# Shared expert's first half: down products of rounded halves, chunk by chunk into four banks, and the first row transposes in the up products' bank

## What is computed

```python
def _L0_ffn_ref(x, Wg, W1, b1, W11, b11, W2, b2, Ws1, bs1, Ws11, bs11, Ws2, bs2):
    ...
    logits = xf @ Wg
    _, topi = jax.lax.top_k(logits, K)
    ...
    z = jax.nn.silu(xf @ Ws1 + bs1) * (xf @ Ws11 + bs11) @ Ws2 + bs2
    return (y + z).reshape(b, t, d)
x = x + jnp.tanh(g_xattn[0]) * _L0_xattn_ref(_layernorm(x, axis=-1), ctx_1024, ctx_1024, ...)
x = x + jnp.tanh(g_ffn[0]) * _L0_ffn_ref(_layernorm(x, axis=-1), L0_ffn_Wg, ...)
```

## Time and profile before

| What | Value |
|---|---|
| Median of three runs | 577.51 us (574.35, 577.51, 577.92) |
| The profiled execution, its time | 574.41 us |
| Its span in the profile | 572.2 us |
| TensorE busy in it | 546.9 us (96%) |
| VectorE, ScalarE, POOL busy | 352.1, 238.2, 335.4 us |
| Mean granted TensorE clock | 0.997 of full speed |

### The profile page before, as it was taken

How to read it: one execution, slowest core, us unless ns; L and a number is a source line. 1 busy time by engine, 2 the same in 40 slices (tenths; PEclk the granted TensorE clock), 3 DMA queues, 4 the chain that set the end, 5 groups by cost and what they waited for, 6 DMA issues and landing times.

```text
span 572.2 us, 12049 instructions
## 1 busy us (share of the span) xinstructions
PE 546.9 (96%) x3290; PEld 442.1 (77%) x3291; DVE 352.1 (62%) x861; ACT 238.2 (42%) x787; POOL 335.4 (59%) x273
## 2 busy tenths in 40 slices
PE   8879999999988999988999999999999999999997
PEld 7546766767757878767888888888888888888886
DVE  6648788778668842145566555665556655535687
ACT  0799899999995211012222212222122221233232
POOL 4588899999864386640374675364454560226660
PEclk9899999999999999999999999999999999999999
DMA  8572001001023044244257868558556210012442
GB/s 282 236 295 80 21 21 37 21 18 37 12 82 111 30 165 175 92 129 175 69 190 262 302 240 302 177 179 289 201 173 258 82 46 29 28 56 84 121 121 89
DMA packets 32898, 76.08 MB, mean 133 GB/s; under 512 B 4960, under 2 KB 21856, under 8 KB 29920
## 3 DMA queue, kind: packets, MB, share of 16 engines
q1 hardware_dynamic: 14960, 52.44, 25.7%
q10 hardware_dynamic: 14832, 14.82, 8.2%
q0 software_dynamic: 3072, 8.39, 4.7%
HBM read 54.93 MB, written 18.61 MB: 129 GB/s over the span
## 4 chain that ended last, share of the span: by engine, by line
PE 85%; ACT 6%; DVE 5%; issue 3%; POOL 0%; ACTq 0%; DVEq 0%; POOLq 0%
PE mid L748 14%; PE big L729 8%; PE big L731 8%; PE big L730 7%; PE big L652 5%; PE big L650 5%; PE big L651 5%; PE big L516 5%; PE mid L739 4%; ACT arena L836 3%; PE mid L529 3%; PE work L548 3%; PE last L541 2%; PE last L669 2%; PE work L669 2%
## 5 line engine op out<-in xcount | busy, mean ns | idle before, releaser
L936 ACT ACTIVATE last<-arena 128x512 f32<-128x512 f32 x47 | 28.3, 602 | 183.4 <-DVE arena L1405 183.4
L836 ACT ACTIVATE arena<-big,nmax 128x128 f32<-128x128 f32 x256 | 90.0, 388 | 1.7 <-DVE nmax L1058 1.5
L748 PE MATMUL mid<-dring,arena 128*128 x376 | 89.0, 379 | 0.0
L1405 DVE TENSOR_TENSOR arena<-big,bring 128x512 f32<-128x512 f32 x47 | 32.5, 692 | 87.3 <-PE big L731 87.3
L729 PE MATMUL big<-u_hi,xsT_hi 128*128 x188 | 81.8, 435 | 1.8 <-issue 1.8
L1568 POOL TENSOR_TENSOR u_lo<-arena,u_hi 128x2048 fp32r<-128x2048 f32 x16 | 74.3, 4645 | 1.3
L748 PEld LDWEIGHTS mid<-dring,arena 128*128 128x128 f32 x376 | 67.8, 190 | 7.3
L731 PE MATMUL big<-u_hi,xsT_lo 128*128 x188 | 73.5, 391 | 0.0
L730 PE MATMUL big<-u_lo,xsT_hi 128*128 x188 | 73.4, 390 | 0.0
L1544 POOL TENSOR_TENSOR arena<-arena,rinv 128x1024 f32<-128x1024 f32 (+1 forms) x32 | 59.4, 1855 | 13.5 <-DVE rinv L1066 13.5
L1668 POOL TENSOR_TENSOR pool_mark<-mhalf 128x1 f32<-128x1 f32 x15 | 2.9, 193 | 104.9 <-PE big L731 88.3
(11 more groups left out here) (197 smaller groups left out, 1203.8 us busy)
## 6 DMA issues: line engine op xcount, KB each, us to landing
arena<-up_w_dram SPq DMA_DIRECT2D x16, 1024.0 KB, 7.6
bring<-expert_bias_dram SPq DMA_DIRECT2D x16, 640.0 KB
dring<-down_w_dram SPq DMA_DIRECT2D x18, 512.0 KB
sorted_y<-arena ACTq DMA_DIRECT2D x47, 128.0 KB, 1.7
arena<-sorted_x ACTq DMA_DIRECT2D x43, 128.0 KB, 2.1
sorted_x<-dring SPq DMA_DIRECT2D x3, 1536.0 KB, 8.5
arena<-ctx_t_dram ACTq DMA_DIRECT2D x8, 256.0 KB, 2.7
dring<-up_w_dram SPq DMA_DIRECT2D x2, 1024.0 KB, 4.9
```

The costliest lines, as they stand in the source:

```text
L748: i = mm(mid[:, 1, 0:D], gT[:, p, c, :], dring[:, slot, c * D:(c + 1) * D], start=(c == 0), stop=(c == HC - 1))
L836: i = nc.scalar.activation(probs[:, u % 2, h, :], big[:, u % 2, h // 4, (h % 4) * CTX:(h % 4 + 1) * CTX], ACT.Exp, bias=nmax[:, u % 2, h:h ...
L1405: v.tensor_tensor(hb1[:, p, :], big[:, p, 0, :], bring[:, slot, 0:HID], ALU.add).then_inc(h1_ready, 1)
```

## The change

In the first half the down products are made as in the second: ScalarE rounds each hidden chunk, VectorE makes the remainder, and TensorE adds 12 products of 256 columns per chunk into four banks (`first_bank`). POOL makes the halves of the first half's down weights ahead of the scatter. The hidden chunks of the first half now go through `gg` (two buffers) in place of `gshT`; the new tiles `first_d` and `first_gs` lie in the region of `arena`. The totals and ranks go to free columns of `mid`, whose banks now hold down sums. TensorE's order becomes up n, down n - 1 (later n - 2). The transposes of the first two blocks of rows go into `big`, the up products' bank, ahead of down chunks 13 to 15, and these come ahead of the first block's up product. Functions common to both halves replace `last_down`; the order of the second half is as it was.

```diff
+        first_d = sb("first_d", [P, 2, DCOLS], F32R)
+        first_gs = sb("first_gs", [P, 2, 2, 512], F32R)
...
+        first_bank = (work, last, mid[:, 0, :], mid[:, 1, :])
+        def hidden_chunk(n):
+            return gg[:, n % 2, :] if n < HC * TILES // GROUP else gshT[:, n // HC % 2, n % HC, :]
+        def rounded_chunk(n):
+            if n < HC * TILES // GROUP:
+                return first_gs[:, 0, n % 2, :], first_gs[:, 1, n % 2, :]
+            return gs_hi[:, n % 2, :], gs_lo[:, n % 2, :]
...
-            def shared_down(s, tiles=range(GROUP)):
...
-                        i = mm(zbank[t % 2][:, 0:D], gshT[:, s % 2, c, t * P:(t + 1) * P], dring[:, slot, c * D:(c + 1) * D],
-                               start=(c == 0), stop=(c == HC - 1))
-                    i.then_inc(z_ps, 1)
+            def shared_down(n):
+                h, c = divmod(n, HC)
...
+                pe.wait_ge(gs_lo_ready, n + 1)
+                if n == 0:
+                    pe.wait_ge(d_split, 1)
+                    pe.wait_ge(lg_taken, PAIRS)
+                    pe.wait_ge(rank_taken, 1)
...
+                for t in range(GROUP):
+                    if c == 0 and h > 0:
+                        pe.wait_ge(z_taken, GROUP * (h - 1) + t + 1)
...
+                    mm(banks[t][:, 0:D], g_hi, w_hi, start=(c == 0), stop=False)
+                    mm(banks[t][:, 0:D], g_hi, w_lo, start=False, stop=False)
+                    i = mm(banks[t][:, 0:D], g_lo, w_hi, start=False, stop=(c == HC - 1))
+                    if c == HC - 1:
+                        i.then_inc(z_ps, 1)
+                    elif t == GROUP - 1:
+                        i.then_inc(gs_used, 1)
...
             shared_up(0, 3)
+            shared_down(0)
             pe.wait_ge(xfT_kept, 4)
...
+            for n in range(4, 8):
+                shared_up(1, n - 4)
+                shared_down(n - 3)
+            shared_down(5)
             pe.wait_ge(xfT_kept, PAIRS)
...
+            for n in range(8, 15):
+                shared_up(n // HC, n % HC)
+                shared_down(n - 2)
...
-            transpose_rows(0, 0)
-            shared_down(3, range(1))
-            transpose_rows(1, 1)
+            shared_up(3, 3)
+            pe.wait_ge(gsh_ready, HC * TILES // GROUP - 1)
+            transpose_rows(0, 0, big[:, 0, 0, :])
+            transpose_rows(1, 1, big[:, 0, 1, :])
+            for n in range(13, 16):
+                shared_down(n)
+            pe.wait_ge(xsT_ready, 2)
+            pe.wait_ge(gsh_ready, HC * TILES // GROUP)
             up(0, 0)
-            pe.wait_ge(xsT_ready, 2)
-            shared_down(3, range(1, GROUP))
-            pe.wait_ge(z_taken, 4 * GROUP)
+            pe.wait_ge(z_taken, TILES)
             transpose_rows(2, 2)
...
+            shared_silu(0, 0)
+            round_hidden(0)
+            shared_silu(0, 1)
+            round_hidden(1)
+            shared_silu(0, 2)
+            for n in range(3, 8):
+                shared_silu(n // HC, n % HC)
+                round_hidden(n - 1)
+            round_hidden(7)
+            for n in range(8, 16):
+                shared_silu(n // HC, n % HC)
+                round_hidden(n)
...
             v.tensor_tensor(gtmp[:, 0, :], top2[:, 1, :], top2[:, 0, :], ALU.subtract).then_inc(gate_exp_in, 1)
+            keep_rest(0)
             shared_hidden(0, [2])
...
             v.tensor_copy(pos[:, :, :], pos_f[:, :, :]).then_inc(pos_ready, 1)
+            keep_rest(1)
             shared_hidden(0, [3])
+            keep_rest(2)
             shared_hidden(1, [0])
+            keep_rest(3)
...
+            for n in range(8, 15):
+                shared_hidden(n // HC, [n % HC])
+                if n % HC == 1:
+                    add_shared(n // HC - 1)
+                keep_rest(n)
+            shared_hidden(3, [3])
+            copy_rows(0, 0, big[:, 0, 0, :])
+            keep_rest(15)
+            copy_rows(1, 1, big[:, 0, 1, :])
+            add_shared(3)
...
+            def split_down(n, source, hi, lo):
+                g.tensor_copy(hi, source).then_inc(d_hi_done, 1)
+                pool.wait_ge(d_hi_done, n)
+                g.tensor_tensor(lo, source, hi, ALU.subtract).then_inc(d_split, 1)
+
+            pool.wait_ge(w_even, 32)
+            pool.wait_ge(pt_ready, 2 * UNITS * PAIRS)
+            split_down(1, dring[:, 0, :], first_d[:, 0, :], first_d[:, 1, :])
             pool.wait_ge(pos_ready, 1)
```

More of the change, by code:

```diff
@@ L148, in flamingo_layer @@
         ARENA = 16128
-        arena = sb("arena", [P, ARENA])
+        with nc.sbuf_tensor("arena", [P, ARENA], F32) as whole:
+            arena = whole
+        first_d = sb("first_d", [P, 2, DCOLS], F32R)
+        first_gs = sb("first_gs", [P, 2, 2, 512], F32R)
+        sb("arena_rest", [P, ARENA - 2 * DCOLS - 4 * 512])
         taken = [0]
@@ L654, in shared_up @@
                     i.then_inc(sh_ps, 1)
[L656 to L671 removed]
+            def shared_down(n):
+                h, c = divmod(n, HC)
+                second = h >= TILES // GROUP
+                banks = last_bank if second else first_bank
+                hi, lo = rounded_chunk(n)
+                d = (d_hi, d_lo) if second else (first_d[:, 0, :], first_d[:, 1, :])
+                pe.wait_ge(gs_lo_ready, n + 1)
[3 more added lines that the diff above has]
+                    pe.wait_ge(rank_taken, 1)
+                if n == HC * TILES // GROUP:
+                    pe.wait_ge(d_split, 2)
+                    pe.wait_ge(g_ready, BLOCKS)
+                    pe.wait_ge(xsT_ready, BLOCKS)
+                    pe.wait_ge(gT_ready, BLOCKS)
+                    pe.wait_ge(y_ready, BLOCKS)
+                for t in range(GROUP):
+                    if c == 0 and h > 0:
+                        pe.wait_ge(z_taken, GROUP * (h - 1) + t + 1)
+                    g_hi, g_lo = hi[:, t * P:(t + 1) * P], lo[:, t * P:(t + 1) * P]
+                    w_hi, w_lo = d[0][:, c * D:(c + 1) * D], d[1][:, c * D:(c + 1) * D]
+                    mm(banks[t][:, 0:D], g_hi, w_hi, start=(c == 0), stop=False)
[5 more added lines that the diff above has]
+                        i.then_inc(gs_used, 1)
@@ L1284, in _, with copy_rows @@
             pair(LAST, 1, False, True, False)
-            def copy_rows(b, p):
+            def copy_rows(b, p, bank=work):
                 dve.wait_ge(xs_ps, b + 1)
@@ L1288, in copy_rows @@
                     dve.wait_ge(up_ps, b - 1)
-                v.tensor_copy(xsT_hi[:, p, :], work[:, 0:D]).then_inc(rows_hi, 1)
+                v.tensor_copy(xsT_hi[:, p, :], bank[:, 0:D]).then_inc(rows_hi, 1)
                 dve.wait_ge(rows_hi, b + 1)
-                v.tensor_tensor(xsT_lo[:, p, :], work[:, 0:D], xsT_hi[:, p, :], ALU.subtract).then_inc(xsT_ready, 1)
+                v.tensor_tensor(xsT_lo[:, p, :], bank[:, 0:D], xsT_hi[:, p, :], ALU.subtract).then_inc(xsT_ready, 1)
             def shared_hidden(s, chunks):
@@ L1310, in add_shared @@
                         dve.wait_ge(combined, min(tile + 1, TILES - GROUP - 1) if g == 2 else tile + 1)
-                    bank = last_bank[t] if h > 0 else zbank[t % 2]
+                    bank = last_bank[t] if h > 0 else first_bank[t]
                     v.scalar_tensor_tensor(out=x_all[:, tile, :], in0=bank[:, 0:D], scalar=tanh_g[:, 1:2],
@@ L1350, in _ @@
             dve.wait_ge(rank_ps, 1)
-            v.scalar_tensor_tensor(out=cnt[:, 0, :], in0=starts, scalar=float(P), in1=mid[:, 0, 0:E], op0=ALU.mult, op1=ALU.add) \
+            v.scalar_tensor_tensor(out=cnt[:, 0, :], in0=starts, scalar=float(P), in1=mid[:, 0, D:D + E], op0=ALU.mult, op1=ALU.add) \
                 .then_inc(rank_taken, 1)
@@ L1433, in _ @@
             add_biases(0, 0)
-            add_shared(3, range(1, GROUP))
             copy_rows(2, 0)
```

120 lines of the change are left out of this document (40 added, 80 removed).

## The result

The changed kernel takes **579.53 us** (20 runs, 576.36 to 584.2), the kernel before beside it 575.74 us (20 runs, 572.98 to 578.92): ratio **1.0068 [1.0046, 1.0090]**, so 4 us slower. The forecast against the first median of 577.51 was 2 us faster, 575.5 us, with a range to 579.0.

A forecast was written before the change was run, and what follows sets the result against it. TensorE's queue bounds the kernel; the scatter has 4.9 us of slack. Scatter late by 2.9 + 2.9 = 5.8 us: transposes 0.9 us later, 2.8 us gained behind them, so about 2 us faster: 575.5 us, range 569.5 to 579.0.

The forecast's parts named there:

- TensorE's work: Ups and downs up to the third row transposes: up 2.75, down 1.43 us; TensorE alone would gain 7.7 us.
- The 1 us at the first reuse of the banks: Ahead of the row transposes: TensorE loses about 1 us because VectorE's four additions are slower than four tiles.
- POOL's first split: First down weights' split from 182.3 us: conflicts with two VectorE operations, delaying everything behind on VectorE by 2.9 us.
- The marks: VectorE operation at 182.64 us, towards the positions: waits for POOL's copy until 183.4, ends at 183.9 us.
- rival C: Slower, 578.5 us: each remainder stops the next indirect DMA, scatter over 7.7 us late; chance with lower clock 0.15.
- Thirteen remainders beside the indirect DMAs: VectorE's remainders during the scatter: each stretches an indirect DMA by 0.22 us, 2.9 us in all.
- rival A: Part of the lateness, POOL's split or the remainders, is missing: gain 4.8 up to 6 us, 571.5 to 572.7; chance 0.22.
- ScalarE is mostly idle here too. Cost nothing: Sixteen added first-half roundings fit under each 4.2 us of TensorE; without that cover, 0.7 us a chunk.
- 9.3 us behind the first transposes: First to third row transposes: 8.9 us plus 0.4 for the second block's rows, against 12.1 before; 2.8 us gained.
- My rule for place 1: At POOL's first split: a two-SBUF-input VectorE operation and a POOL operation reading SBUF wait each other out.
- The scatter as the bound: Before the row transposes: scatter 5.8 us late, slack 4.9; rows land at 251.4 us, TensorE waits 3.2 us.
- The three signs that I named for being wrong: Positions not late, the 32 indirect DMAs keeping their mean, or no TensorE wait before the row transposes.

The follow-up runs named there:

- e11: e8 with the 32 indirect DMAs replaced by plain DMAs to fixed rows, token sorting left out: 565.01 us, 0.9833 of the kernel before.
- e14: e10 with the 32 indirect DMAs replaced by plain DMAs to fixed rows, token sorting left out: 565.62 us, 0.9875 of the kernel before.
- e6: The kernel before with the 32 indirect DMAs replaced by plain DMAs to fixed rows, token sorting left out: 573.89 us, ratio 0.9972.
- e10: e4 with, from chunk 8 on, ScalarE's silu n ahead of rounding n - 1, VectorE's hidden n ahead of remainder n - 1: 567.78 us, ratio 0.9893.
- e5: The changed kernel with the 32 indirect DMAs replaced by plain DMAs to fixed rows, token sorting left out: 572.90 us, 0.9961 of the kernel before.
- e4: The changed kernel with POOL's first split earlier and its second split waiting for all sixteen remainders and the gates: 572.49 us, 0.9955 of the kernel before.
- e8: e4 with TensorE at up n, down n - 3, ScalarE silu n, rounding n - 1, VectorE hidden n, remainder n - 1: 570.74 us, ratio 0.9944.
- e7: The changed kernel with fp32 first-half downs again (no roundings, remainders or down-weight split), new order and banks kept: 569.15 us, 0.9899 of the kernel before.

## Why the prediction was wrong, point by point

- **TensorE's work: the pace right, its worth a little too large.** Up at 2.75 and down at 1.43 us to the hundredth. Of 7.7 us in all, e11 and e14 against e6 measured 8.0 and 5.6, their traces 6. The 250.54 us from which the forecast subtracted held late signals too: e6 reaches its first transposes 65.6 us behind POOL's last rstd, the kernel before 68.8. The 1 us at the first reuse of the banks was not there (downs 4 and 5 took 2.87 together).
- **POOL's first split: mechanism right, term too small.** The marks ended within 0.2 us of the forecast. But the positions came 4.0 us late, not 2.9. The sum passed 2.9 us on to TensorE for its router, and went no further: TensorE idled 2.1 us there and its clock fell, which rival C had only put at the rows, and hidden chunk 2, ahead of the positions, waited for the slow up product. "VectorE has no idle time there" was not quite so either: it had 0.61 us before that chunk, at 190.15 us. Put back into e10 the split costs 4.9 us.
- **Thirteen remainders beside the indirect DMAs: term too large.** The 32 took 1023 ns each against 997, 0.83 us in all, not 2.9. A remainder costs only if it is already running when a DMA begins, as rival A had said ("0 to 1 us in all"). Of the changed kernel's timelines, one such pair and one in which the DMA began first:

```profile
233.70 0.69 DVE L1317 TENSOR_TENSOR first_gs<-arena,first_gs 128x512 fp32r<-128x512 f32 x1
233.85 1.38 POOL L1681 DMA_INDIRECT sorted_x<-xf_all,pos  x1 [0.31 <-issue]
...
248.34 0.96 POOL L1681 DMA_INDIRECT sorted_x<-xf_all,pos  x1 [0.30 <-issue]
248.70 0.69 DVE L1317 TENSOR_TENSOR first_gs<-arena,first_gs 128x512 fp32r<-128x512 f32 x1 [3.54 <-ACT first_gs L931]
```

  Only three of its eleven remainders beside the scatter met a DMA in this way. By the rule that the forecast set aside (the Trainium skill, "SBUF — State Buffer", "Who interferes with whom": tensor_tensor does not hold up the writing of descriptors) the term is 0. That is nearer in number, but these traces don't agree with the rule. In e10 it was 1062 ns, 2.1 us.
- **"ScalarE is mostly idle here too. Cost nothing": the step that failed first.** By its busy time this holds. But TensorE's signals came up to 6.7 us late, a late signal delays what stands in ScalarE's queue, and the added rounding put a second such wait into that queue, ahead of the next silu. TensorE lost 6.6 us in this stretch of the changed kernel's trace, none there in e5's, and the other order of silu and rounding alone gives 3.6 us (e4 to e10). The trace of before showed late silus already (that of 220.94 us had 2.94 us of idle ahead of it, where e6 has 2.03); none of them was in my rows.
- **"9.3 us behind the first transposes": the second step that failed.** 13.55 us. The parts of the sum were right (e10 takes 254.87 - 245.51 = 9.36), but I followed POOL's queue only to the scatter's end. Before, the split behind it (243.71 to 250.29 us) met no VectorE operation with two SBUF inputs; the change put the last remainder there. My rule for place 1, applied once more, would have found it.
- **The scatter as the bound: did not come to it.** Rows at 254.5, aligned 250.4 (forecast 251.4), but TensorE came at 259.0, aligned 255.0. Freed of its own waits, in e10, it does wait for them.
- **Rivals.** C was the right side by another mechanism; its own, every remainder stopping the next DMA, did not happen. A's was right for the remainders and wrong for the time. The three signs that I named for being wrong: the positions were late, the mean hardly moved, and no wait came before the transposes: the last two said so.

## What to carry to other kernels

When a change adds operations with two SBUF inputs to VectorE, go through every POOL operation that reads SBUF up to the end of the changed stretch, old ones too, and give POOL a wait that keeps it out of the way. An engine that is idle half the time can still be on the path: count how many waits for another engine's signal its queue has between two steps, and put the work that the bounding engine waits for ahead of them. e10 does both and is 1.07% under the kernel before, where the change was 0.68% over. The second advice rests on e4 against e10 alone; e8 follows it too and is not told apart from e4. And try the parts of a change apart: e7, the new order with the old products, is as fast as e10 and needs none of this.

## What the runs showed of the hardware that was not expected

- TensorE's completion signals come up to 6.7 us late beside indirect DMAs, also in bursts, while the products go on at their pace; with plain DMAs of the same bytes and packets, in a shorter scatter, they come within 0.02 us. It is there beside POOL's gathers in the last stretch too: in the changed kernel an up ends at 540.25 and its silu starts at 542.05.
- An indirect DMA that begins while a VectorE tensor_tensor with two SBUF inputs is running ends 0.83 to 0.84 us after it, in 60 of 61 cases in 13 traces (one 0.89; the first DMA of each scatter, 0.25 us longer by itself, left out). All others took 0.96 to 1.01 us, also when such an operation began after them.
- VectorE operations with a single SBUF input are held by POOL too: TENSOR_SCALAR on 128x16 took 3.92 us beside a POOL subtraction (0.23 for the one behind it).
- After 2.09 us of idle TensorE's clock was 0.56 and 0.59 in the next two windows of 2 us; in e10, after 2.4 us of idle ahead of the transposes, the window 246 to 250 us had 1.00. The length of the pause alone doesn't tell.
